# Two attentions of a five-stage kernel rebuilt: heads weighed four at a time, stacks for all images in one copy, a causal mask without matmuls

## The reference

```python
x = _L0_conv_ref(x, ...)
x = x + _L1_conv_ref(_gn(x), ...)
t = _to_tokens(x)
t = t + _L2_attn_ref(_ln_t(t), w_qkv, w_proj, b_proj)      # 16 heads of 16
t = t + _L2_ffn_ref(_ln_t(t), gate_w, w1, w2, w3)          # 8 experts, top 2, hidden 512
t = t + _L3_attn_ref(_ln_t(t), Wq, Wk, Wv, Wo, bo)         # the same, causal
t = t + _L3_ffn_ref(_ln_t(t), Wg, W1, W2, W3)              # 8 experts, top 2, hidden 1024
return _from_tokens(t, x)

def _L3_attn_ref(x, Wq, Wk, Wv, Wo, bo):
    q, k, v = heads(x @ Wq), heads(x @ Wk), heads(x @ Wv)
    scores = jnp.einsum('bhqd,bhkd->bhqk', q, k)
    scores = jnp.where(jnp.tril(ones), scores, -jnp.inf)
    attn = jax.nn.softmax(scores / np.sqrt(16), axis=-1)
    return (attn @ v, heads merged) @ Wo + bo
```

## Time and profile before

| | us |
|---|---|
| three runs, median (lowest to highest) | 1068.17 (1067.59 to 1070.4) |
| profiled execution | 1069.0 |
| its span, first to last instruction | 1067.2 |
| a2: layer norm to last residual | 267.8 to 410.5 |
| f2 | 411.4 to 600 |
| a3 | 602.9 to 745 (normalising from 600.6 on) |
| f3 | 746.7 to 1067.2 |

### The profile page before, as it was taken

One profiled execution on the slowest core, in us unless ns is written; L12 is line 12 of the kernel. 1 busy time (PEld: TensorE's weight loads), 2 busy tenths in 40 slices (PEclk: granted clock), 3 DMA queues, 4 the chain that ended last, 5 costly groups with the idle time before them and its releaser, 6 DMA issues. The chain is left out here.

```text
span 1067.2 us, 12919 instructions
## 1 busy us (share of the span) xinstructions
PE 877.1 (82%) x4252; PEld 555.6 (52%) x4253; DVE 452.5 (42%) x937; ACT 295.6 (28%) x446; POOL 204.1 (19%) x280
## 2 busy tenths in 40 slices
PE   4678389898768996399999378998379999999994
PEld 2666246336434554166565245665346666666662
DVE  4973522897546433522222555551622122122122
ACT  3223336431324351021221133333112222222221
POOL 1240000770001000233343101000111211211210
PEclk7589579999869996599999689998579999999997
DMA  3000060000347202032111334850202205710103
GB/s 105 1 1 1 19 228 1 0 1 1 88 117 193 66 1 87 15 106 96 49 41 38 129 95 145 208 149 1 87 20 68 100 20 189 312 40 20 29 15 128
DMA packets 53771, 80.26 MB, mean 75 GB/s; under 512 B 10297, under 2 KB 46141, under 8 KB 50525
## 3 DMA queue, kind: packets, MB, share of 16 engines
q1 hardware_dynamic: 48192, 67.25, 20.1%
q0 software_dynamic: 5536, 12.46, 3.8%
HBM read 55.69 MB, written 11.27 MB: 63 GB/s over the span
## 5 line engine op out<-in xcount | busy, mean ns | idle before, releaser
L1996 PE MATMUL psum<-ring,f_x_t 128*128 x552 | 253.8, 603 | 1.3 <-DVE f_x_t L1864 1.3
L1857 DVE TENSOR_TENSOR f_gated<-f_silu,psum 128x512 f32<-128x512 f32 x69 | 47.4, 687 | 270.4 <-PE psum L1996 270.4
L1996 PEld LDWEIGHTS psum<-ring,f_x_t 128*128 128x128 f32 x552 | 101.4, 194 | 104.3 <-issue 104.2
L2010 PE MATMUL psum<-ring,f_gated_t 128*128 x552 | 130.7, 380 | 1.8 <-ACT f_gated_t L1923 1.8
L2010 PEld LDWEIGHTS psum<-ring,f_gated_t 128*128 128x128 f32 x552 | 101.2, 190 | 23.5 <-issue 12.8
L1282 DVE TENSOR_REDUCE a_maxima<-psum 128x2 f32<-128x512 f32 x128 | 82.9, 687 | 61.5 <-PE psum L1440 32.2
L1923 ACT ACTIVATE f_gated_t<-psum 128x512 f32<-128x512 f32 x69 | 41.2, 597 | 236.6 <-PE psum L2003 236.6
L1919 ACT ACTIVATE f_silu<-psum 128x512 f32<-128x512 f32 x69 | 41.2, 597 | 113.6 <-PE psum L1996 113.6
L1374 ACT ACTIVATE a_expo<-psum 128x1024 f32<-128x1024 f32 (+1 forms) x64 | 58.3, 911 | 40.6 <-PE psum L1471 24.5
L1437 PE MATMUL psum<-a_stack_k,a_stack_q 96*128 96x256 bf16 (+1 forms) x256 | 49.7, 277 | 20.9 <-DMA a_stack_k<-a_parts 11.8
L1489 PE MATMUL psum<-a_expo,a_values 128*32 128x256 f32 (+1 forms) x512 | 61.3, 358 | 0.0
(11 more groups left out here) (294 smaller groups left out, 1232.0 us busy)
## 6 DMA issues: line engine op xcount, KB each, us to landing
ring<-in_f_experts SPq DMA_DIRECT2D x24, 1536.0 KB, 7.7
a_stack_q<-a_parts SPq DMA_DIRECT2D x96, 64.0 KB, 2.9
a_stack_k<-a_parts SPq DMA_DIRECT2D x96, 64.0 KB, 2.9
rows_in<-h SPq DMA_DIRECT2D x4, 1024.0 KB, 6.8
ring<-rows_out SPq DMA_DIRECT2D x8, 512.0 KB, 5.4
a_wqkv<-in_a_wqkv SPq DMA_DIRECT2D x2, 768.0 KB
x_in<-in_x SPq DMA_DIRECT2D x1, 1024.0 KB, 4.9
out<-x SPq DMA_DIRECT2D x4, 256.0 KB, 2.1
```

Source lines behind the costliest of these rows:

```text
L1857: dve.tensor_tensor(gated[:, b, :], silu[:, b, :], psum[:, 2 * b + 1, :], ALU.mult).then_inc(s_g, 1)
L1996: last = pe.matmul(psum[:, 2 * b + side, :], x_t[:, xb, t, :], k.ring[:, bass.ds(at + start, CHUNK)], start=(t == 0), stop=(t == CT - 1))
L2010: last = pe.matmul(psum[:, Y_BANK, 0:C], gated_t[:, b, P * a:P * a + P], k.ring[:, bass.ds(at + start, C)], start=(c == 0 and a == 0), sto ...
```

## The change

- **Weights of attention** (`wqkv`, `w_proj`, `b_proj`) lie in shared tensors and are loaded by SP in the block before (`load_next`): a2's in the scan, a3's in f2. The bias is replicated on 128 partitions and added to `t` by POOL once, before the loop; the one-row matmuls go.
- **Layer norm image by image**, in all four places: statistics of image 0, then for each image the statistics of the next and its own normalising. In attention PE projects the first half of the tokens for q and k between the transposes; ACT alone copies the transposed images. The order of the splits changes so that q and k alternate.
- **Stacks for all four images**: one DMA moves 256 KB in 2 KB rows, 12 for the first heads and 12 for the last, all ahead of the loop; nothing is loaded in the loop. The stacks of the last heads lie in the second half of the experts' ring. The rows of negated maxima are issued by SP, behind these.
- **Values of four heads** are weighed together, after every second unit, with four buffers of exponentials (two in `k.h`): keys outermost, the four heads, each with its own 32 PSUM partitions, innermost.
- **Causal mask**: in the maxima, DVE adds a matrix `later` and reduces in one operation, two for each head (128 and 256 keys); behind the exponential, POOL zeroes later keys (`affine_select`), and `weigh_values` waits for that. All ban matmuls go.
- **Ring**: three of six chunks (`EARLY_CHUNKS`) are loaded early; the other three at the start of the experts' block, behind the store of the normalised tokens. Before the first gathers DVE's table gets two more small steps.

```diff
+        def stacks(half, which):
+            return (stacks_low, stacks_high)[half][:, which]
...
-            for i in range(2 * CT):
-                t, which = i // 2, i % 2
-                for part, done in enumerate((s_hi, s_mid, s_lo)):
-                    sp.wait_ge(done, i + 1)
+            for t in range(CT):
+                for which, part, done in ((0, 0, s_hi), (1, 0, s_hi), (0, 1, s_mid), (0, 2, s_lo), (1, 1, s_mid), (1, 2, s_lo)):
+                    sp.wait_ge(done, 2 * t + which + 1)
                     for c, combo in enumerate(COMBOS):
                         if combo[which] == part:
-                            for b in range(2):
-                                sp.dma_start((stack_q, stack_k)[which][HD * c:HD * c + HD, 2 * t + b],
-                                             parts[:, t, which, part, N * b:N * b + N]).then_inc(s_first[t], 16)
+                            sp.dma_start(stacks(t, which)[HD * c:HD * c + HD], parts[:, t, which, part, :]).then_inc(s_st[t], 16)
...
+            for g in range(GROUPS):
+                sp.wait_ge(s_nl, g + 1)
+                sp.wait_ge(s_nh, g + 1)
+                for q in range(MAXROWS):
+                    sp.dma_start(group_stack(g, 0)[STACK + q:STACK + q + 1], negated[:, g % SLOTS_G, q, :]).then_inc(s_mr[g % 2], 16)
                 prefetch(sp, g)
...
+            pool.tensor_tensor(k.t[:], k.t[:], b_proj[:].unsqueeze(1).broadcast_to([P, TT, C]), ALU.add).then_inc(s_bias, 1)
+            def zero_future(i):
+                pool.wait_ge(s_ex, i + 1)
+                on_diagonal = exponentials(i).rearrange("p j (m n) -> p j m n", m=NT)[:, :, :, 0:P]
+                pool.affine_select(on_diagonal, on_diagonal, [[0, 2], [0, NT], [1, P]], ALU.is_ge, 0.0, base=0,
+                                   channel_multiplier=-1).then_inc(s_sel, 1)
...
+                if causal:
+                    for t in range(NT):
+                        keys = P * t + P
+                        last = dve.tensor_tensor_reduce(masked[:, i % 2, t, 0:keys], psum[:, i % 2, N * t:N * t + keys],
+                                                        later[:, N - keys:], 1.0, -3e38, ALU.add, ALU.max,
+                                                        maxima[:, g, t, h:h + 1])
...
-                        if causal:
-                            last = pe.matmul(psum[:, bank, col:col + P], ident16[:], bans[:, 1, :], start=False, stop=True)
...
-            def weigh_values(i):
-                pe.wait_ge(s_ex, i + 1)
+            def weigh_values(quad):
+                pe.wait_ge(s_sel, 2 * quad + 2)
...
-                for j in range(2):
-                    h = 2 * unit + j
-                    q, col = 32 * (h % 4), N * (h // 4)
-                    for m in range(NT):
+                for m in range(NT):
+                    first = n1 if m else 0
+                    for lane in range(4):
+                        h = 4 * (quad % QUADS) + lane
...
-                    last = pe.matmul(out, ones[:], b_proj[:], start=False, stop=True)
...
+            sp.wait_ge(s_loaded, 16 * EARLY_CHUNKS)
+            for n in range(EARLY_CHUNKS, RING_CHUNKS):
+                load_chunk(sp, k, w["experts"], chunks, n, s_loaded)
+            load_next(sp)
```

More of the change, by code:

```diff
@@ L1154, in sm @@
             return sem(f"{tag}_{name}")
[L1156 to L1161, removed]
+        wqkv, w_proj, b_proj = k.wqkv, k.w_proj, k.b_proj
+        if causal:
+            later = sb("later", [P, N])
+            masked = sb("masked", [P, 2, NT, N], BF16)
         h_t = k.x1[:].rearrange("p t b n -> p t (b n)")
@@ L1217, in _ @@
         def _(sp):
[L1218 to L1230, removed]
@@ new lines, in _ @@
+            for t in range(CT):
+                for which in range(2):
+                    source = psum[:, 2 * which:2 * which + 2, :].rearrange("p a n -> p (a n)")
+                    dve.wait_ge(s_hi, 2 * t + which + 1)
+                    if t:
+                        dve.wait_ge(s_lo, which + 1)
+                    dve.tensor_tensor(rest[:, which, :], source, parts[:, t, which, 0, :], ALU.subtract).then_inc(s_r, 1)
+                for which in range(2):
+                    dve.wait_ge(s_mid, 2 * t + which + 1)
+                    dve.tensor_tensor(parts[:, t, which, 2, :], rest[:, which, :], parts[:, t, which, 1, :],
+                                      ALU.subtract).then_inc(s_lo, 1)
@@ L1384, in _, with turn_image @@
         def _(pe):
-            for i in range(TT // 2):
+            def turn_image(i):
                 pe.wait_ge(ln.s_out, 2 * i + 2)
@@ L1414, in project_values @@
                     last.then_inc(s_v, 1)
-            for T in range(TT // 2):
+            turn_image(0)
+            turn_image(1)
+            pe.wait_ge(w["loaded"], 16 * 3)
+            pe.wait_ge(s_hto, 2)
+            for which in range(2):
+                project_half(0, which, 0)
+            turn_image(2)
+            turn_image(3)
+            pe.wait_ge(s_hto, 4)
+            for which in range(2):
+                project_half(0, which, 1)
+            for T in range(2):
+                project_values(T)
+            for which in range(2):
+                pe.wait_ge(s_r, which + 1)
+                for half in range(2):
+                    project_half(1, which, half)
+            for T in range(2, VALUES_BEFORE):
                 project_values(T)
@@ L1553 @@
 RING_CHUNKS = 6
+EARLY_CHUNKS = RING_CHUNKS // 2
 PAIRED = (MAXBLK + 1) // 2 * 2
@@ L2134, in _host_arrays @@
     above = np.where(order[None, :] > order[:, None], forbid, 0.0)
-    a["bans"] = np.stack([above, above.T, np.full((P, P), forbid)], 1).astype(bf16)
-    a["ident16"] = np.eye(P).astype(bf16)
+    a["later"] = np.concatenate([np.zeros((P, P)), above], 1).astype(np.float32)
     def dims_outermost(m):
```

244 lines of the change are left out of this document (125 added, 119 removed).

## The result

| | before | changed |
|---|---|---|
| runs, median (lowest to highest), us | 1067.88 (1066.76 to 1070.4), 4 runs | 1084.22 (1083.37 to 1087.64), 4 runs |
| profiled execution, its span | 1069.0, 1067.2 | 1084.0, 1082.2 |
| a2 | 143.7 | 153.4 |
| f2 | 189.2 | 189.6 |
| a3 | 146.1 | 148.5 |

The changed kernel is slower: ratio to the kernel before 1.0153, 95% interval 1.0129 to 1.0177. The forecast was 1043 us, faster. A block is counted here from SP's first issue in it to SP's first issue in the next.

The account below looks back on a forecast made before the run. PE was taken to bound the attention loops, stack landing their start, and matmuls the experts' blocks. From 1069.0 us, -15 -5.6 (a2), -16 -5.6 (a3), +12.2 (starts), +4 (experts) gave -26: 1043 us, range 1012 to 1095.

Parts of the forecast that it names:

- the deciding number: Start of both attentions: cost of one 256 KB stack copy, taken as 1.41 us; said to move the time most.
- Stacks: Start of each attention: 24 stack copies of 1.41 us take 33.8 us, so the first unit starts 6.1 us later.
- the sum: All terms from 1069.0 us: -15 -5.6 (a2), -16 -5.6 (a3), +12.2 (two starts), +4: -26, giving 1043 us.
- the rival: Both starts: copies land at one 16-partition set's rate, down to 93 GB/s, 2.82 us each; 1110 us; chance 0.27.
- the row of 186: Earlier trace: small stack copies queued behind a ring load moved 186 GB/s, all engines occupied; taken as 1.41 us a copy.
- Start of the copies: Start of each attention: copies start some 3 us later, from projection order 1.8 us and layer norm about 1.5 us.
- Values: a2's loop: four heads run side by side, a quad costs 0.99 us like a unit; saves 15 us.
- Bias: Projections: dropping the one-row bias matmuls saves 1.4 us in each of four, 5.6 us in each attention.
- Mask: a3's loop: without bans, and with four-head values, a group falls from 10.44 to 8.4 us, saving 16 us.
- Loops together: Loops of both attentions: savings from values, bias and mask together, 42.2 us.
- Experts' blocks: Both experts' blocks: gate 1 us later in each, first gather slowed by late ring loads; 4 us longer for both.
- The signposts that decide: Profile rows: 186 GB/s (rival 100), first unit 54 us after block start (rival 85 to 90), a2 group 8.1 us.

Follow-up runs that it names:

- the experiment: Changed kernel plus a last block that only copies; 24 copies of 64 KB in 512 byte rows, queued behind a 1.5 MB load, moved 164 GB/s over 4 us.

## Why the prediction was wrong

It read the bound rightly and named the deciding number rightly ("What a copy costs is the open number"), and took the wrong value for it.

- **Stacks: the step that failed.** 1.41 us a copy was read from the earlier trace rows, a burst of 2.2 us in which 64 KB copies in 512 byte rows were queued. Over 4 us the same form gave 164 GB/s in the experiment, 1.60 us for 256 KB, so about a quarter of the miss lies in the short reading and the rest in the form. The argument that "it is this queued state that the new copies are in" was taken from the state of the queue and not from the form of the copies. Measured, 24 copies take 53.9 us in a2 and 53.3 in a3, 2.24 each. That is 20.1 us more in each attention than the 33.8 of the sum. The point given for the rival, 1.96 us a copy, held: 48 copies times 0.28 us above it are 14 us, the loss is 15. The rival had the right mechanism (16 partitions in turn took 117 GB/s, the same 16 three times 112: the rate is that of one set) and overshot at 2.82 us. The 104 GB/s of the Trainium skill (SBUF — State Buffer, section on Door 1: the DMA port swizzle), by which the prediction estimated about 1095, was nearer to 1084 than either; the prediction itself said that the row of 186 doesn't refute it, and still took that row.
- **Start of the copies.** Forecast 3 us later, measured 4.9. Part of it is probably the clock: PE's first eight matmuls of the projection ran at a granted clock of 0.56 (274.9 to 281), most of them 0.85 us apart instead of 0.43, after transposes with idle time between them. Before, only the first two starts were that far apart, so the difference is about 2 us, an estimate from these starts. The experiment with the whole norm, and the old order of transposes, gives back all 4.9. POOL's addition of the bias, which falls there, is not the cause: without it (the bias undone) the copies start at 18.5 and 17.5 us, as in the changed kernel (18.5 and 17.7). With the copies: 6.1 + 20.1 + 1.9 = 28.1 us forecast after correction, 27.2 and 26.7 measured. In a2 the way from the first issue to the first packet and from the last packet to the first unit took 2.4 us, for which the sum had 3.2.
- **Values.** 15 us in a2 forecast, 12.3 measured by undoing; the packing (1.00 us a quad) was exact. But with it undone a group takes 9.81 us, 1.66 more, and not the 1.98 of two units of 0.99. In a3 7.8; PE isn't alone in setting the pace there, and what else does wasn't measured apart.
- **Bias.** 5.6 forecast, 7.8 and 7.5 measured: 1.55 us for each projection where 1.4 was taken, and more at the end of the block.
- **Mask.** The group was forecast at 8.4 us and came to 7.61: a head's two reductions take DVE 0.57 us from the first to the next head's, not 0.85, and the selection 0.64, not 1.27. What that is worth in time is another matter: what bans cost in this loop was overrated. The 16 us of the sum held a3's values too; undone apart, values and mask are 7.8 and 5.8, together 13.6. The undone parts add to 21.1 us in a3, with 24.2 measured and 21.6 in the sum.
- **Loops together.** 41.7 us less, 42.2 forecast, and that is luck: a2 gave 17.5 instead of 20.6, a3 24.2 instead of 21.6. After the long wait the first three units of a2 ran at a granted clock of 0.50 (8.6 us, the second window above), 2.66 us apart where two later ones are 1.84 apart; by an estimate from these starts, about 2.5 us that a late start costs on top. Before, the first 8.6 us of that loop had 1.00.
- **Experts' blocks.** 4 us forecast, 3.1 measured (0.4 and 2.7).
- **Sum with the measured terms:** 1069.0 + 27.2 + 26.7 - 17.5 - 24.2 + 0.4 + 2.7 = 1084.3, measured 1084.0. All of them are differences of the two traces, so this checks the bookkeeping and no cause.

The signposts that decide read as promised: 118 GB/s, a start of 74.9 us (forecast 54, rival 85 to 90), a period of 8.15. Two smaller ones missed: DVE's maxima are 0.57 us a head apart, not 0.75, and the gate of f2 starts 0.5 us later after its block's start, not 1. The chances that the prediction lists for faster add to 0.71, not to its 0.68. The range of 1012 to 1095 held the time; the sign was wrong.

## What to carry to other kernels

A rate read from a queue belongs to the form that was queued: source, destination partitions, size and row length; and a reading over 2 us can be high even for that form. Before a plan moves megabytes inside SBUF, look which partitions each copy writes; where a matmul sums over rows, their order is free, and a stride that spreads them may raise the rate for one changed slice, here from 118 to 225 GB/s. When a gain in the loop is large and certain, ask how much the start may lose before it is gone, and measure that one number by itself: twelve copies in a block of their own tell it.

## What was not expected of the hardware

- 16 rows side by side took 117 GB/s and the same rows six partitions apart 219; 32 rows four apart reached 376, what 128 do (380).
- 64 neighbours took 131 GB/s from 128 partitions of SBUF, 236 from DRAM and 238 from themselves.
- A memset of 6.93 us on POOL stretched an operation of two elements on DVE from 0.17 to 7.65 us.
- Rows of 4 KB on POOL's queue needed 13.0 us to land beside queued copies of the SP queue; over the whole of that run the median is 1.6, and it was 3.0 in the kernel before.
